# A recurrence with its bonus term and value split moved one stage ahead, two fill banks, and five row products in three short passes

## The reference, cut to what matters

```
def step(s, inp):
    k_l, v_l, w_l, r_l = inp
    a = k_l[..., :, None] * v_l[..., None, :]
    out = jnp.einsum('bhs,bhst->bht', r_l, faaaa * a + s)
    return a + w_l[..., None] * s, out
...
x = x + y * g @ Wo.T
...
rr = jax.nn.sigmoid(xr2 @ fWr.T)
kk = jnp.square(jax.nn.relu(xk2 @ fWk.T))
x = x + rr * (kk @ fWv.T)
```

## Time and profile before

| | |
|---|---|
| runs of the kernel before | 3117.07 us median of 3, 3107.01 to 3122.32 |
| the profiled execution, its own time | 3116.61 us |
| its span, first to last instruction | 3114.5 us |
| mean granted TensorE clock | 0.924 of full speed |
| busy share of the span | PE 85%, DVE 47%, ACT 35%, POOL 39% |
| first scan to last output of the recurrence | 611.5 to 941.4 us |
| the five row products | 328, 973, 1024, 1081 and 1250 us, 28 to 30 us each |

### The profile page before, as it was taken

How to read it: one execution, slowest core, us unless ns; L and a number is a source line. 1 busy time by engine, 2 the same in 40 slices (tenths; PEclk the granted TensorE clock), 3 DMA queues, 4 the chain that set the end, 5 groups by cost and what they waited for, 6 DMA issues and landing times. The chain is left out here.

```text
span 3114.5 us, 38784 instructions
## 1 busy us (share of the span) xinstructions
PE 2655.3 (85%) x14106; PEld 2266.8 (73%) x14106; DVE 1456.8 (47%) x2524; ACT 1104.9 (35%) x2344; POOL 1227.3 (39%) x601
## 2 busy tenths in 40 slices
PE   4888468778897888799699999979998699999699
PEld 2666133367773346499589999869998699999599
DVE  1656441289894222431256666443111456656443
ACT  0767021212212101221266666432111566565321
POOL 2000122266661000341297877543100778777210
PEclk9999768899998899899799999989999799999899
DMA  4543131323221014172444444246322544443210
GB/s 134 136 107 84 37 138 77 120 71 101 97 78 48 1 54 153 68 271 96 161 151 150 145 151 150 75 145 214 123 97 106 190 142 157 150 139 112 84 55 22
DMA packets 208336, 357.22 MB, mean 115 GB/s; under 512 B 85316, under 2 KB 126684, under 8 KB 206996
## 3 DMA queue, kind: packets, MB, share of 16 engines
q1 hardware_dynamic: 208148, 354.75, 34.8%
HBM read 261.16 MB, written 99.61 MB: 116 GB/s over the span
## 5 line engine op out<-in xcount | busy, mean ns | idle before, releaser
L1577 PE MATMUL ca_ring<-ca_pp,ca_xh 128*128 128x400 f32 (+1 forms) x1536 | 405.5, 345 | 0.0
L1577 PEld LDWEIGHTS ca_ring<-ca_pp,ca_xh 128*128 128x128 f32 (+1 forms) x1536 | 286.2, 190 | 0.2
L1577 PE MATMUL ca_ring<-ca_pp,ca_xl 128*128 128x400 f32 (+1 forms) x768 | 268.4, 349 | 17.8 <-POOL ca_xl L1987 9.9
L1977 POOL TENSOR_TENSOR ca_kl<-ca_kl,ca_kh 128x1448 fp32r<-128x1448 f32 x64 | 211.8, 3310 | 170.8 <-ACT ca_kh L2018 170.8
L1577 PE MATMUL qk_bank<-qk_ch,qk_wl 128*128 128x362 f32 x768 | 252.5, 329 | 0.0
L1577 PE MATMUL qk_bank<-qk_ch,qk_wh 128*128 128x362 f32 x768 | 251.7, 328 | 0.0
L1577 PE MATMUL qk_bank<-qk_cl,qk_wh 128*128 128x362 f32 x768 | 251.4, 327 | 0.0
L2106 DVE TENSOR_TENSOR ca_yl<-ca_ring,ca_yh 128x400 fp32r<-128x400 f32 x256 | 146.4, 572 | 183.7 <-ACT ca_yh L2044 183.7
L1987 POOL TENSOR_TENSOR ca_xl<-state_X,ca_xh 128x1536 fp32r<-128x1536 f32 x64 | 226.5, 3539 | 5.0
L1577 PE MATMUL ca_score<-ca_kh,ca_q 128*100 128x362 f32 x512 | 150.1, 356 | 64.4 <-POOL ca_kl L1977 46.2
L1754 DVE TENSOR_SCALAR qk_stage<-qk_bank,qk_columns 128x361 f32<-128x361 f32 x96 | 56.8, 593 | 314.4 <-PE qk_bank L1577 300.2
(11 more groups left out here) (362 smaller groups left out, 6674.1 us busy)
## 6 DMA issues: line engine op xcount, KB each, us to landing
ca_kl<-keys SPq DMA_DIRECT2D x64, 724.0 KB, 5.1
keys<-qk_stage SPq DMA_DIRECT2D x48, 724.0 KB, 3.1
state_X<-in_ctx SPq DMA_DIRECT2D x64, 512.0 KB, 3.8
queries<-qk_stage SPq DMA_DIRECT2D x16, 1600.0 KB
ca_q<-queries SPq DMA_DIRECT2D x64, 400.0 KB, 3.9
state_X<-in_ctx SPq DMA_DIRECT2D x64, 210.0 KB, 4.3
rec_fcl<-fill_ctxT SPq DMA_DIRECT2D x16, 724.0 KB, 4.4
keys<-rec_stage SPq DMA_DIRECT2D x64, 181.0 KB, 1.9
```

Source lines behind the costliest of these rows:

```text
L1577: issued = nc.tensor.matmul(out, x, y, start=(first and k == 0), stop=(last and k == count - 1))
L1977: nc.gpsimd.tensor_tensor(kl[:, n % 2].bitcast(F32R), kl[:, n % 2], kh[:, n % 2].bitcast(F32), ALU.subtract).then_inc(k_ready, 1)
```

## The change

It does these things:

1. The bonus term and the split of the value leave the recurrence. `gate_and_present` computes them in the gate's block, for all batches, and writes three tensors of 1.6 MB to DRAM (`kept_value_high`, `kept_value_low`, `kept_present`); `kept_value` is no longer written. The recurrence loads them.
2. The matrix `spread` is loaded as it is used, without a rounding, from a DRAM copy that the layer's first copies make.
3. Fills take two banks in turn, begin in slot 10 and are spread over 118 slots. Both weight groups of a batch are done before the next batch, so a context comes in once. A finished group of four heads is written by one DMA.
4. GpSimd's low parts are made in quarters, one after a multiply.
5. The four loads of l1y are issued from within the recurrence.
6. `product_rows` splits both operands (weight in four chunks, source batch by batch in a ring of three) and issues three fp32r matmuls where one fp32 matmul stood.

Fills in the recurrence (cut):

```diff
+            slots = B * HD - FROM
+            if slot < FROM:
+                return range(0)
+            return range((slot - FROM) * FILL * CC // slots, (slot - FROM + 1) * FILL * CC // slots)
...
+            def store(m):
+                b, g, _ = fill_place(m * G3)
+                sp.wait_ge(fill_kept, G3 * (m + 1))
+                sp.wait_ge(learned, m + 1)
+                sp.dma_start(keys[g * B + b], stage[:, m % 2]).then_inc(stored[m % 2], 16)
...
-            for b in range(B):
-                if b and b + 1 < B:
+            for tile, src in later:
+                sp.dma_start(tile, src).then_inc(later_in, 16)
+            for b in range(1, B):
+                store(FILLED_GROUPS * (b - 1))
+                if b + 1 < B:
                     load(b + 1)
-                for u in range(PER * b, PER * (b + 1)):
-                    store(u)
-                    if u % G3 == G3 - 1 and u // G3 + 2 < FILL // G3:
-                        load_context(u // G3 + 2)
-            for h in range(G3):
-                sp.wait_ge(stored[h], 16 * (FILL // G3))
+                    load_context(b + 1)
+                store(FILLED_GROUPS * (b - 1) + 1)
...
+                last = products(nc, fbank[u % 2][:, 0:SP], [((fwh[:, g, c, part], fwl[:, g, c, part].bitcast(F32R)),
+                                                            (fch[:, b % 2, c, :], fcl[:, b % 2, c, :].bitcast(F32R)))],
+                                first=c == 0, last=c == CC - 1)
+                if c == CC - 1:
                     last.then_inc(fill_full, 1)
...
+                    for chunk in fill_chunks(HD * b + j):
+                        fill(chunk)
```

GpSimd and VectorE in the recurrence:

```diff
+            aside = {}
+            for c in range(CC):
+                aside[1 + c] = (low_weights, 0, c)
+                aside[1 + CC + c] = (low_context, 0, c)
+                aside[1 + 2 * CC + c] = (low_weights, 1, c)
+                for b in range(1, B):
+                    aside[BATCH * b + 4 + c] = (low_context, b, c)
...
-                    if j % STEP == STEP // 2 - 1:
-                        low_context((HD * b + j) // STEP + 1)
-                    if b == 0 and j % 4 == 2 and 1 <= j // 4 + 1 < FILLED_GROUPS:
-                        low_weights(j // 4 + 1)
+                    if HD * b + j in aside:
+                        split, i, c = aside[HD * b + j]
+                        split(i, c)
...
+            def finish(b):
+                dve.wait_ge(now_in[b % 2], 16 * (b // 2 + 1))
+                dve.wait_ge(gathered, HD * (b + 1))
+                nc.vector.tensor_tensor(out[:, b], sumb[b % 2][:, :, 0:L], now[:, b % 2], ALU.add).then_inc(out_done, 1)
...
+                for j in range(HD):
+                    column(b, j)
+                    if b and j == 3:
+                        finish(b - 1)
+            finish(B - 1)
```

The new function, cut, and its surroundings:

```diff
+def gate_and_present(nc, prefix, weight, source, gate, blocks, key, value, receive, bonus, high, low, ruk, a, kept):
...
+            def present(b):
+                pe.wait_ge(ruk_done, CC)
+                if b >= 4:
+                    pe.wait_ge(now_done, b - 3)
+                nc.tensor.matmul(nbank[b % 4][:, :, 0:L], blocks[:], ruk[:, b], start=True, stop=True).then_inc(now_full, 1)
...
+                    last = nc.tensor.matmul(pbank[u % 4][:, :, 0:L], weight[:, c, n * P:(n + 1) * P],
+                                            source[:, 4 * half:4 * half + 4, c, :], start=(c == 0), stop=(c == CC - 1))
+                last.then_inc(full, 1)
+                if u >= 2:
+                    present(u - 2)
+            present(B - 2)
+            present(B - 1)
...
+            for c in range(CC):
+                nc.vector.scalar_tensor_tensor(ruk[:, :, c, :], receive[:, :, c, :], bonus[:, c:c + 1], key[:, :, c, :],
+                                               ALU.mult, ALU.mult).then_inc(ruk_done, 1)
...
+                dve.wait_ge(high_done, b + 1)
+                nc.vector.tensor_tensor(low[:, b], value[:, b], high[:, b], ALU.subtract).then_inc(low_done, 1)
+            for b in range(B):
+                dve.wait_ge(now_full, b + 1)
+                nc.vector.tensor_tensor(ruk[:, b], nbank[b % 4][:, :, 0:L], value[:, b], ALU.mult).then_inc(now_done, 1)
...
+        def _(act):
+            for b in range(B):
+                nc.scalar.activation(high[:, b].bitcast(F32R), value[:, b], ACT.Copy).then_inc(high_done, 1)
...
+            for name, tile, done in (("value_high", high, high_done), ("value_low", low, low_done), ("present", ruk, now_done)):
+                a[f"kept_{name}"] = nc.dram_tensor(f"kept_{name}", tuple(tile.shape), F32).ap()
+                sp.wait_ge(done, B)
+                sp.dma_start(a[f"kept_{name}"], tile[:]).then_inc(kept, 16)
...
+            a["spread_copy"] = nc.dram_tensor("spread_copy", (P, HD, P), F32).ap()
+            start_copies(nc, "l1f", filled, [(a["spread_copy"], a["spread"]), (a["fill_weights"], a["L3_xattn_wk1"][:, 0:FILLED_GROUPS * W3]), (a["fill_ctxT"], a["ctxT"])])
...
-            keep_in_dram(nc, "value", value, a, kept)
             await_copies(nc, "l1uw", (decay_kept, 1))
-            start_copies(nc, "l1x", matrices, [(spread[:], a["spread"]), (gather[:], a["gather"]), (blocks[:], a["blocks"])])
+            await_copies(nc, "l1ux", (filled, 3))
+            start_copies(nc, "l1xb", blocks_in, [(blocks[:], a["blocks"])])
+            start_copies(nc, "l1x", matrices, [(spread[:].bitcast(F32), a["spread_copy"]), (gather[:], a["gather"])])
             mix_and_product(nc, "l1u", mixing(4, mix[1]), (CC, dense(W["WrT"], mix[0]), keep(receive)))
             keep_in_dram(nc, "receive", receive, a, kept)
-            mix_and_product(nc, "l1v", None, (CC, dense(W["WgT"], mix[1]), keep(gate, ACT.Silu)))
-            await_copies(nc, "l1k", (kept, 3), (matrices, 3), (filled, 2))
+            await_copies(nc, "l1vw", (blocks_in, 1))
+            gate_and_present(nc, "l1v", W["WgT"], mix[1], gate, blocks, key, value, receive, col("faaaa"), cur, diff, mix[0], a, kept)
+            await_copies(nc, "l1k", (kept, 5), (matrices, 2))
```

`product_rows` (the function's prefix is that of the caller):

```diff
             for b in range(B):
+                pe.wait_ge(source_low, b + 1)
                 for c in range(CC):
-                    last = nc.tensor.matmul(banks[b][0:L, :], source[:, b, c, :], weight[:, c, :],
-                                            start=(c == 0), stop=(c == CC - 1))
+                    if b == 0:
+                        pe.wait_ge(weight_low, c + 1)
+                    last = products(nc, banks[b][0:L, :], [((sh[:, b % RING_S, c, :], sl[:, b % RING_S, c, :]), (wh[:, c, :], wl[:, c, :]))],
+                                    first=c == 0, last=c == CC - 1)
                 last.then_inc(full, 1)
 
-        if engine_name == "vector":
-            @block.vector
-            def _(dve):
+        @block.gpsimd
+        def _(pool):
+            for b in range(B):
+                pool.wait_ge(source_high, b + 1)
+                nc.gpsimd.tensor_tensor(sl[:, b % RING_S], source[:, b], sh[:, b % RING_S].bitcast(F32), ALU.subtract).then_inc(source_low, 1)
+
+        @block.vector
+        def _(dve):
+            for c in range(CC):
+                dve.wait_ge(weight_high, c + 1)
+                nc.vector.tensor_tensor(wl[:, c, :], weight[:, c, :], wh[:, c, :].bitcast(F32), ALU.subtract).then_inc(weight_low, 1)
+            if aside:
+                aside()
+            if engine_name == "vector":
                 for b in range(B):
                     dve.wait_ge(full, b + 1)
...
+            def high_source(b):
+                if b >= RING_S:
+                    act.wait_ge(full, b - RING_S + 1)
+                nc.scalar.activation(sh[:, b % RING_S], source[:, b], ACT.Copy).then_inc(source_high, 1)
+
+            high_source(0)
+            for c in range(CC):
+                nc.scalar.activation(wh[:, c, :], weight[:, c, :], ACT.Copy).then_inc(weight_high, 1)
+            for b in range(1, RING_S):
+                high_source(b)
+            for b in range(B):
+                if b + RING_S < B:
+                    high_source(b + RING_S)
```

More of the change, by code:

```diff
@@ L772, in _, with recurrence @@
                 product[2](act, n, half, pbank[u % 4][0:product[1](n, half)[0][0].shape[-1], :, 0:L]).then_inc(kept, 1)
-def recurrence(nc, key, value, decay, receive, first, bonus, spread, gather, blocks, out, weights, ctxT, head_columns, keys):
+def recurrence(nc, key, decay, receive, value_high, value_low, present, first, spread, gather, out, weights, ctxT, head_columns, keys, later, later_in):
     N = CC * L
     AHEAD = 4
-    EARLY = 3
     FILL = FILLED_GROUPS * B * G3
-    PER = FILL // B
-    SLOTS_PER = HD // PER
+    FROM = 10
+    BATCH = HD - 1
     with Scope(nc, "rec") as sc:
-        kb, vb, wb, rb = (sc.sb(n, [P, 2, CC, L]) for n in ("kb", "vb", "wb", "rb"))
+        kb, wb, rb = (sc.sb(n, [P, 2, CC, L]) for n in ("kb", "wb", "rb"))
         vh, vl = sc.sb("vh", [P, 2, CC, L], F32R), sc.sb("vl", [P, 2, CC, L], F32R)
```

(16 more changed lines are left out.)

256 lines of the change are left out of this document (115 added, 141 removed).

## The result

The changed kernel takes 3069.41 us (median of 4 runs, 3063.64 to 3080.33) where the kernel before takes 3116.5 (4 runs, 3107.01 to 3122.32): a ratio of 0.985, with a 95% interval of 0.9827 to 0.9873. The forecast was 3075 with a range of 3055 to 3100. The profiled execution took 3069.59 us, its span 3067.5, against 3114.5 before.

A forecast was written before the change was run, and what follows sets the result against it. It took VectorE's scan paired with GpSimd's multiply, and TensorE nearly equal, to bound the recurrence. Recurrence -40, row products -12, gate stage with detour +11.4 and smaller terms gave -42 us, from 3116.6 to 3075; range 3055 to 3100.

The forecast's parts named there:

- Steady batches: Recurrence, six batches after the first: each falls from 39.2 to 34.3 us, a gain of 29 us in all.
- floor of 34.0: Recurrence: TensorE's slots of 2.12 us make 34.0 us a batch, below which a batch can't go.
- 32.2 us for the pair: Recurrence: VectorE's scan and GpSimd's multiply take turns; with splits and waits removed, they need 32.2 us a batch.
- GpSimd waits in line: Rival, recurrence: GpSimd's context piece waits for ScalarE's rounding and stops the multiplies; 3100 us in all, chance 12%.
- Neither hides the other: Rival, recurrence: scan and multiply and TensorE slip only so far against each other; 36.4 us a batch, 3091 in all, 17%.
- First batch: Recurrence, from first scan to first copy: falls from 53 to 46 us, a gain of 7 us.
- Last batch and tail: Recurrence's end, 42 us to the last output: gains 4 us from one split less and two fill banks.
- Gate stage: Stage ahead of the recurrence: eight head sums on TensorE add 5.4 us, the detour through DRAM 6, between 2 and 12.
- First load to first scan: Start of the recurrence, 10.9 us before: 2.5 us less, between 0 and 4, as roundings and a subtraction go.
- SyncE's blocks and the DRAM copy of `spread`: Blocks where only SyncE works add 1.2 us; the copy issued ahead of the layer's first block adds 1, between 0 and 6.
- Row products: Five row products, short passes in place of fp32 matmuls: 12 us less together, between 0 and 20.
- Slower clock: Rival, recurrence: TensorE stays at 1.2 GHz when fills begin, 4.24 us a slot; 3322 us over all 118 slots, chance 3%.

## Why the prediction was right, and where its steps were not

The direction and the order of limits held: the pair of scan and multiply was relieved, and TensorE came next. That the total came within 6 us is luck in part. In the recurrence two misses cancelled: six steady batches gained 9.5 us too little, the first batch 9 too much. The wait that the sum left to a rival with 12% was there all the same. Point by point:

- **Steady batches**: forecast 34.3 us, measured 35.9; the six gave -19.5 in place of -29. The floor of 34.0 was right to 0.1 us (34.07 with early rounding, 33.96 without the splits). The 32.2 us for the pair don't fit their own rates: 16 slots of 1.96 and 3.76 of pieces are 35.1, above TensorE's floor. What saves the floor is that a piece adds 0.65, not 0.94: 16 x 1.96 + 4 x 0.65 = 34.0. What failed is the step that took 34.3 and left GpSimd's wait to a rival. "GpSimd waits in line" came true in its mechanism and at half its price: 12 us, where 3 in seven batches and 4 in the first were priced. "Neither hides the other" gave 36.4 us a batch, near the 35.9 measured, but its mechanism is refuted by the early rounding: with all the pieces in place and no wait, a batch takes 34.07 us and TensorE is busy 35.00 of 35, so one hides the other.
- **First batch**: forecast 46 us, measured 36.9 between first scan and copy, -16.2 in place of -7. Two steps were oversized. A quarter does not add its whole length to a slot. Its duration of 1.65 us is in good part a hold: it starts at 742.78, the scan of 742.12 ends at 743.66, and the piece ends at 744.43, 0.77 us later. A slot with a piece is 2.6 us, 0.65 more than 1.96, where I had counted 0.94 on paper. And the copy is VectorE's place, which runs ahead of the rest; by first outputs, it gained 13.1 us (61.3 to 48.3 from the first scan).
- **Last batch and tail**: forecast -4, measured -0.6 from the copy, -2.9 from the last output but one.
- **The parts of the recurrence** were summed on the wrong engine. I charged the gain to work taken off VectorE and GpSimd and, in the tail, 4 us to the second bank. The runs show that no one part carries it. Without the bank, a batch goes back to 39.06, by itself nearly the whole gain. With a whole split it goes to 38.2. Without the bonus term but with all else old, nothing is gained. These prices don't add up to the 3.3 us gained a batch, since each is what is lost when one part alone is undone. The old bonus term in the changed kernel was not run, so what its removal is worth there is open.
- **Gate stage**: +5.4 exact; the round trip 5.0 of 6. l1y -2.1 exact, seen again where the first load comes 1.25 us behind the stage. First load to first scan -3.6 of -2.5, within its bounds.
- **SyncE's blocks and the DRAM copy of `spread`**: forecast +2.2, measured -0.6, below what can be told.
- **Row products**: -11.6 of -12. The pass takes 0.231 us, the row's 0.233. The estimate of 216 ns by the Trainium skill ("TensorE: Matmul & The Clock Gate", "Back-to-back issue gap") was 7% short. The same section calls its formula the isolated gap and gives some 131 ns as sustained for 512 columns, which is further off: the passes here average 231. The sum of 3067 that went with the 216 came near the time for another reason, since the row products gave 12 us and not 20. The start took 2.3 to 2.7 us of splits, 2.4 forecast; the first dozen passes of l0o took 0.43 us each, at the lower clock.
- **Slower clock**: in the first batch the grant was 0.73 while GpSimd was full, and 1.00 in the steady batches. It cost nothing: in the run with fp32 row products the same 37 us from the first scan had a mean grant of 0.77, here 0.69, and both take 36.9 us.

The lock between VectorE and GpSimd is what the earlier trace rows showed, and it holds in both directions: a piece that starts just ahead of a scan takes 0.95 us and the scan beside it 1.78, a piece that starts behind one takes 1.65. The first of these, from the changed kernel's timeline of GpSimd and VectorE:

```profile
844.60 0.95 POOL L969 TENSOR_TENSOR rec_fcl<-rec_fcl,rec_fch 128x362 fp32r<-128x362 f32 x1
844.62 1.78 DVE L1009 TENSOR_TENSOR_SCAN rec_state<-rec_wb,rec_rank 128x400 f32<-128x400 f32 x1
```

The Trainium skill says so ("SBUF — State Buffer", "SBUF: two separate sides"): the shared pair is an exclusive lock for a whole instruction, and the other engine blocks. By these rows the trace agrees. I had read it off for the scan only, and took the length of GpSimd's instructions as fixed. Its multiply has a mean of 1251 ns in the earlier trace rows and takes 1.05 us at 741.77, so the holds stood in a row that I had.

## What to carry to other kernels

When a stage has two engines near full and a third that feeds them, work out the floor of each and look for what waits in line between them, since the time landed there in this case. A change of the order of one engine's program by a few instructions (rounding earlier: 12 us; head sums earlier: 5 us; the pass that needs no low part first: 5 us) gave 22 us together by their stages, half of what the whole rewrite gave. An instruction that waits in an in-order program stops all behind it: put it where its input has been ready for a while, and look at every round trip through memory for work of the same stage that could stand behind its start. And before a part of a gain is credited to one edit, take that edit alone in both directions.

## What was not expected of the hardware

- With less work (no bonus term), the old recurrence was not faster: 1.0032 (1.0019 to 1.0044).
- The same recurrence code took 330 and 344 us in two profiles, and stages of unchanged code differ by up to 22 us between executions, while 21 runs of the kernel before, taken together, lie between 3103.5 and 3130.3 us, within 0.9%. A gain of 10 us has to be read from its own stage.
- 512 columns in fp32r take 0.231 us a pass from one to the next at the full clock, 400 columns 0.182: 0.45 ns a column in both.
